# A normalised input written once by VectorE, its two parts formed by GpSimd ahead of slot 1, and a wait moved ahead of the experts

## The chip, the cores and the metric

One Trainium2 chip, one core of it. The metric is the time of one execution in microseconds (us). The engines run their own instruction streams side by side and wait for one another on semaphores: TensorE (PE) for matrix products into the accumulator memory PSUM, VectorE (DVE), ScalarE (ACT) and GpSimd (POOL) for elementwise work, SyncE (SP) for the DMA queue between HBM and the on-chip memory SBUF.

## What is computed

A block of three residual parts over 16 images of 64 channels by 256 positions: a graph convolution over the whole batch, a gated state-space scan over the positions, and a mixture of eight experts of which two count for each position. Cut to the last two, which the change touches:

```
t = t + scan(ln(t))                            # a recurrence over 256 positions, 128 channels x 16 states
logits = ln(t) @ Wr + br ; probs = softmax(logits) ; top_p, top_idx = top_k(probs, 2)
weights = top_p / top_p.sum(-1)
xn = (xt - mean) * rsqrt(var + eps)            # xt = ln(t)
h = gelu((xn * ln_g[e] + ln_b[e]) @ W1[e] + b1[e]) ; y[e] = h @ W2[e] + b2[e]     # e = 0..7
t = t + sum over the two chosen e of weights[e] * y[e]
```

## The kernel before

The kernel is written engine by engine, with every wait by hand; the order of each engine's stream is the order of its code. Two images, one of each half of the batch, are worked on at a time, 64 channels of each on 128 partitions, in G = 8 rounds. Round i runs the scan of pair i, the experts of the pair before (prev), and the input work of the two pairs after (nxt, nxt2). The loops are the four functions named body, one per engine; they call the same helpers in a fixed order.

The scan of a pair is cut into eight slots. dve_slot multiplies the input of two blocks into PSUM (L810) and runs the recurrence (L816) into the ring hs; pool_slot on GpSimd multiplies the result by Cs (L353, 128x1024); pe_sum adds four slots' worth on TensorE (L1117). When all slots are summed, dve_gate (L837) writes ygs, TensorE projects it, and dve_t1 (L841) makes t1, the state ahead of the experts. These are done one round later, between slot 0 and slot 1 of the next pair.

The layer norm ahead of the experts follows slot 1 on VectorE. dve_lnF (L847) writes tns for the router; dve_xn2 writes the experts' input. That input, X2, is held as a high part rounded to the matrix product's type and a low part, the rest, which are laid over each other on 128 partitions: the high part on partitions 0 to 63 (L862, for each half), the low part on 64 to 127 (L397, on GpSimd, from the unrounded copy xnt2 of L854). Both halves of the batch lie side by side in its 512 columns. The weights W1H and W1L stand on both halves of the partitions, so it does not matter on which half a part lies. The low part waits for both halves of the high part, for slot 1 of GpSimd and for the experts of the pair before.

dve_router1 (L867, L870) takes logits from PSUM; ScalarE makes their exponentials (act_router, L656); dve_router2 (L878 to L899) finds the two best. Its instructions from L890 on read small tiles in SBUF, rt and rv. After L899 GpSimd makes the weights (pool_router, L403 to L414), which TensorE transposes (pe_wt).

On TensorE, pe_spread (L1209) copies steps for the scan's decay, then one warm matmul (pe_warm, L1296), whose result nobody reads, waits for X2's low part (xl2), then come pe_c and the experts: pe_f1 (L1265, L1266), Gelu on ScalarE (L680, after loading its table at L731), pe_f2 (L1280). Behind the experts come pe_b (L1171, L1173), which waits until VectorE's slot 7 has read the old content, pe_dtz and the pe_sum's. step_input on GpSimd (L338, L340) writes what SP then stores to HBM and loads back for the next pair.

The last pair has its own path behind the loops: VectorE writes the low part itself (L1100).

Of the kernel before, what the change touches and what calls it, by code (L numbers as in the profile page):

```python
# [24 lines left out]
B, D, HW = 16, 64, 256  # L25
HALF = B // 2
G = HALF
T = 2 * HW
# [6 lines left out]
SLOTS = NBLK // 2  # L35
CHUNKS = 4
BY_PE = (8, 9, 10, 11, 12, 13, 14, 15)
EXP, FH = 8, 256
# [32 lines left out]
def build(nc, x, cW1, cb1, Wl, bl, Wr, Wf, bf, cW2, cb2, W_in, b_in, W_conv, b_conv, A_log, W_bc, b_bc,  # L71
# [10 lines left out]
    with ctx:  # L82
        def sb(name, shape, dt=fp32):
            return ctx.enter_context(nc.sbuf_tensor(name, shape, dt))
# [3 lines left out]
        def since(eng, name, count):  # L88

            if count <= 0:  # L90
                return
            eng.wait_ge(S[name], count)

        def so_far(g, ahead):

            return min(g + ahead, G)
# [69 lines left out]
        rs2 = sb("rs2s", [128, HW])  # L166
        rqs = sb("rqs", [128, HW])
        tns = sb("tns", [128, HW])
        xnt2 = sb("xnt2", [64, T])
        X2 = sb("X2", [128, T], f32r)  # L170
        rt = sb("rt", [128, 12, 4, EXP])
        rv = sb("rv", [128, 8, 4])
# [159 lines left out]
        def step_input(eng, by, g, p):  # L332

            eng.wait_ge(S["sp_ln"], g + 1)
            eng.wait_ge(S["sp_relu"], g + 1)
            since(eng, "dt_out", 16 * (g - 1))
            since(eng, "dlo", g - 1)
            by.tensor_tensor(dts[:, p, :], rl[:, :], sp[:, :], ALU.add).then_inc(S["dt"], 1)  # L338
            eng.wait_ge(S["dt"], g + 1)
            by.tensor_tensor(u[:, :], dts[:, p, :], xc[:, p, :], ALU.mult).then_inc(S["u"], 1)  # L340
# [50 lines left out]
        def pool_x2(eng, g):  # L391

            eng.wait_ge(S["xn2"], 2 * (g + 1))
            eng.wait_ge(S["xh2"], 2 * (g + 1))
            eng.wait_ge(S["cm"], min(SLOTS * (g + 1) + 2, SLOTS * G))
            since(eng, "acc", EXP * g)
            gp.tensor_tensor(X2[64:128, :], xnt2[:, :], X2[0:64, :], ALU.subtract).then_inc(S["xl2"], 1)  # L397

        def pool_router(eng, g):

# [16 lines left out]
        def _(eng):  # L417
# [79 lines left out]
            def body(i, p, nxt, nxt2, prev):  # L497
# [11 lines left out]
                    pool_restart(eng, 0, 1)  # L509
                if nxt is not None:  # L510
                    step_input(eng, gp, nxt, q)
                pool_slot(eng, i, p, 1)
                if prev is not None:
                    pool_x2(eng, prev)
                    pool_router(eng, prev)
                pool_slot(eng, i, p, 2)
                pool_slot(eng, i, p, 3)
# [331 lines left out]
        def dve_xn2(eng, g, between=None):  # L849
            eng.wait_ge(S["rq"], g + 1)  # L850
            since(eng, "xl2", g)
            for h in range(2):
                q = slice(64 * h, 64 * h + 64)
                v.tensor_tensor(xnt2[:, HW * h:HW * h + HW], P[q, XB, 0:HW], rqs[q, :], ALU.mult).then_inc(S["xn2"], 1)  # L854
            if between is not None:
                between()
            since(eng, "f1", EXP * KC * g)
            for h in range(2):
                q = slice(64 * h, 64 * h + 64)
                if h == 1 and between is None:  # L860
                    dve_router1(eng, g)
                v.tensor_tensor(X2[0:64, HW * h:HW * h + HW], P[q, XB, 0:HW], rqs[q, :], ALU.mult).then_inc(S["xh2"], 1)  # L862

        def dve_router1(eng, g):
            logits = P[:, XC, 0:4 * EXP].rearrange("p (c e) -> p c e", e=EXP)
# [55 lines left out]
        def _(eng):  # L921
# [127 lines left out]
            def body(i, p, nxt, nxt2, prev):  # L1049
# [16 lines left out]
                dve_slot(eng, i, 1)  # L1066
                if prev is not None:
                    dve_lnF(eng, prev)
                    dve_xn2(eng, prev)
                    dve_router2(eng, prev, nxt2)  # L1070
                dve_slot(eng, i, 2)
                if i == 0:
# [24 lines left out]
            dve_t1(eng, G - 1, 1)  # L1097
            dve_xn2(eng, G - 1, lambda: dve_lnF(eng, G - 1))
            eng.wait_ge(S["xh2"], 2 * G)
            v.tensor_tensor(X2[64:128, :], xnt2[:, :], X2[0:64, :], ALU.subtract).then_inc(S["xl2"], 1)  # L1100
            dve_router1(eng, G - 1)
            dve_router2(eng, G - 1)
            for e in range(EXP):
# [195 lines left out]
        def _(eng):  # L1299
# [121 lines left out]
            def body(i, p, nxt, nxt2, prev):  # L1421
# [23 lines left out]
                pe_spread(eng, i, 14)  # L1445
                pe_spread(eng, i, 15)
                if prev is not None:
                    eng.wait_ge(S["xl2"], prev + 1)
                    pe_warm(eng, 1 if nxt is not None else 2, XB)
                if nxt is not None:  # L1450
                    pe_c(eng, nxt)
                if prev is not None:
# [79 lines left out]
```

## Time and profile before

| | us |
|---|---|
| median of three runs | 395.5 |
| the three runs | 395.0, 395.5, 399.7 |
| the profiled execution, its own time | 399.41 |
| its span in the profile | 397.7 |
| busy: TensorE | 332.3 |
| busy: VectorE | 325.8 |
| busy: ScalarE | 277.2 |
| busy: GpSimd | 267.7 |

The span is the part of an execution that the profiler covers, from the first instruction to the last. Busy time is what an engine's instructions took; waits are not in it. A time for one instruction is given as start and length, both in us from the span's start; a bracket behind it says how long the engine stood before it, and which instruction ended that. Instructions of one engine overlap by up to 0.1 us, since the next one's start is recorded while the last one ends. The granted clock of TensorE is given as a share of 2.4 GHz; it has two levels, 2.4 and 1.2 GHz, so 0.9 is a mean over a stretch. The whole span has 0.924.

### The profile page before, as it was taken

What the parts mean: (1) busy time and instruction counts of PE and PEld (TensorE: products, weight loads), DVE (VectorE), ACT (ScalarE), POOL (GpSimd) and SP (SyncE); (2) the same over time, 40 slices, a digit from 0 to 9 for tenths busy, and PEclk for the clock granted to TensorE, in tenths of its full rate; (3) what the DMA queues carried; (4) which work ended last, traced back from release to release, by engine and by line L of the source; (5) the groups of instructions that cost most, each with busy time, mean ns of one, the idle gap of its engine ahead of it and who ended that gap; (6) DMA issues with size and microseconds to landing.
All of it is one profiled execution on the core that took longest, in us unless ns stands there. A gap on an engine that the chain in (4) does not pass through costs nothing. (4 is left out here: it accounts for less than half of the span.)

```text
span 397.7 us, 5508 instructions
## 1 busy us (share of the span) xinstructions
PE 332.3 (84%) x1674; PEld 182.6 (46%) x1674; DVE 325.8 (82%) x428; ACT 277.2 (70%) x465; POOL 267.7 (67%) x255
## 2 busy tenths in 40 slices
PE   0695897487899889987997899789869987999794
PEld 0475445232555345534544464445345524555462
DVE  2777466998899999989999999899999989993411
ACT  1002557589888977899789778997996778661462
POOL 8803503797569967985699589858985895692122
PEclk9996999559899969999999899999987997899698
DMA  7753059899899888859775997589859960000000
GB/s 190 221 118 47 2 140 217 208 222 223 205 218 232 200 214 208 178 129 226 171 176 140 228 210 177 129 188 221 190 126 216 220 163 3 2 2 13 0 0 15
DMA packets 21302, 59.54 MB, mean 150 GB/s; under 512 B 4989, under 2 KB 13337, under 8 KB 15385
## 3 DMA queue, kind: packets, MB, share of 16 engines
q1 hardware_dynamic: 20104, 58.35, 63.6%
q10 hardware_dynamic: 1168, 0.84, 0.9%
q8 instruction: 14, 0.23, 0.3%
q14 instruction: 16, 0.12, 0.1%
HBM read 53.94 MB, written 5.24 MB: 149 GB/s over the span
## 5 line engine op out<-in xcount | busy, mean ns | idle before, releaser
L353 POOL TENSOR_TENSOR hs<-hs,Cs 128x1024 f32<-128x1024 f32 x63 | 149.6, 2377 | 40.3 <-DVE hs L816 39.7
L816 DVE TENSOR_TENSOR_SCAN hs<-av,P 128x1024 f32<-128x1024 f32 x64 | 146.3, 2286 | 6.2 <-PE P L1117 2.9
L680 ACT ACTIVATE hb<-P,b1c 128x512 f32<-128x512 f32 x128 | 81.5, 686 | 21.3 <-PE P L1266 20.9
L810 DVE TENSOR_TENSOR P<-P,ub 128x1024 f32<-128x1024 f32 x62 | 76.0, 1226 | 3.2 <-DMA ub<-u_scratch 0.9
L1280 PE MATMUL P<-hb,W2s 128*64 128x256 f32 x512 | 69.9, 396 | 0.0
L1265 PE MATMUL P<-X,W1H 128*128 128x512 f32 x128 | 61.4, 480 | 2.4 <-ACT hb L680 2.3
L1266 PE MATMUL P<-X,W1L 128*128 128x512 f32 x128 | 53.9, 421 | 0.0
L617 ACT ACTIVATE av<-P,Aneg 128x510 f32<-128x510 f32 x68 | 43.7, 683 | 6.7 <-POOL rl L340 3.5
L1280 PEld LDWEIGHTS P<-hb,W2s 128*64 128x64 f32 x512 | 31.8, 138 | 31.2 <-issue 21.4
L617 ACT ACTIVATE av<-av,Aneg 128x510 f32<-128x510 f32 x60 | 38.3, 707 | 0.3 <-DMA av<-dt_scratch 0.2
L1209 PE MATMUL P<-D,selD 128*128 128x512 f32 x64 | 30.6, 521 | 9.1 <-ACT av L617 6.7
L1265 PEld LDWEIGHTS P<-X,W1H 128*128 128x128 f32 x128 | 26.1, 204 | 21.1 <-ACT hb L680 14.2
L1117 PE MATMUL P<-hs,selS 128*32 128x512 f32 x256 | 30.2, 598 | 2.1 <-POOL hs L353 2.1
L673 ACT ACTIVATE wbs<-P 128x512 f32<-128x512 f32 x32 | 19.1, 598 | 15.3 <-PE P L1245 15.3
L1266 PEld LDWEIGHTS P<-X,W1L 128*128 128x128 f32 x128 | 26.6, 208 | 5.2 <-issue 2.3
L367 POOL TENSOR_TENSOR accs<-accs,mes 128x512 f32<-128x512 f32 x21 | 26.9, 1283 | 2.4 <-DVE mes L917 2.4
L1296 PE MATMUL P<-W1H 128*128 128x512 f32 x47 | 17.2, 464 | 8.2 <-POOL X L397 8.2
L1209 PEld LDWEIGHTS P<-D,selD 128*128 128x128 f32 x64 | 12.7, 205 | 21.7 <-issue 20.4
L917 DVE TENSOR_TENSOR mes<-P,wbs 128x512 f32<-128x512 f32 x28 | 18.7, 667 | 0.2 <-PE P L1280 0.2
L1117 PEld LDWEIGHTS P<-hs,selS 128*32 128x32 f32 x256 | 6.9, 109 | 23.4 <-issue 12.7
L907 DVE SCALAR_TENSOR_TENSOR mes<-P,cols,wbs 128x256 f32<-128x256 f32 x8 | 3.5, 479 | 16.7 <-PE P L1280 8.8
L389 POOL TENSOR_TENSOR D<-dts,D 64x512 fp32r<-64x512 f32 x8 | 10.2, 1274 | 7.8 <-ACT D L600 6.9
(214 smaller groups left out, 522.1 us busy)
## 6 DMA issues: line engine op xcount, KB each, us to landing
ub<-u_scratch SPq DMA_DIRECT2D x31, 1024.0 KB, 10.8
av<-dt_scratch SPq DMA_DIRECT2D x15, 1024.0 KB, 7.1
dt_scratch<-dts SPq DMA_DIRECT2D x7, 256.0 KB, 2.8
u_scratch<-rl SPq DMA_DIRECT2D x7, 256.0 KB, 2.8
av<-in_L_conv_Wr SPq DMA_DIRECT2D x2, 576.0 KB, 7.0
av<-in_L_conv_Wl SPq DMA_DIRECT2D x2, 576.0 KB, 7.6
res<-in_x SPq DMA_DIRECT2D x4, 256.0 KB, 4.6
hb<-in_L_ffn_W SPq DMA_DIRECT2D x2, 512.0 KB, 5.8
```

The lines of the kernel that those rows point to most:

```text
L353: gp.tensor_tensor(hs[:, at, :, :], hs[:, at, :, :], rep(Cs[:, p, :], 1, 2), ALU.mult).then_inc(S["cm"], 1)
L367: done = gp.tensor_tensor(acc[:, :, :], prev, mes[:, at:at + 2, :], ALU.add)
L617: a_.activation(steps, dt_of, ACT.Exp, scale=Aneg[:, m:m + 1]).then_inc(S["aexp"], 1)
L673: a_.activation(wbs[:, 2 * r:2 * r + 2, :].rearrange("p e f -> p (e f)"), P[:, YS, :], ACT.Copy).then_inc(S["wb"], 1)
L680: a_.activation(hb[:, r % 4, :], P[:, (XA, XB)[r % 2], :], ACT.Gelu, bias=b1c[:, r:r + 1]).then_inc(S["gl"], 1)
L810: v.tensor_tensor(ring, rep(P[:, BB, :], 1, 2), ub[:, 2 * n:2 * n + 2, :], ALU.mult).then_inc(S["bm"], 1)
L816: v.tensor_tensor_scan(hs[:, (SLOTS * g + n) % RING].rearrange("p a t -> p (a t)"), av[:, 2 * n:2 * n + 2, :].rearrange("p a t -> p (a t)" ...
L1117: last = pe.matmul(P[32 * q:32 * q + 32, YS, :], selS[:, k, :], hs[:, (SLOTS * g + n) % RING, q % 2, :], start=(k == 0), stop=(k == 3))
L1209: pe.matmul(P[:, (YS, XA)[m % 2], :], selD[:, m - BY_PE[0], :], D2[:, :], start=True, stop=True).then_inc(S["dt_pe"], 1)
L1265: pe.matmul(P[:, bank, :], W1H[:, e, 128 * k:128 * k + 128], X2[:, :], start=True, stop=False)
L1266: pe.matmul(P[:, bank, :], W1L[:, e, 128 * k:128 * k + 128], X2[:, :], start=False, stop=True).then_inc(S["f1"], 1)
L1280: last = pe.matmul(P[64 * h:64 * h + 64, (XC, XD)[pair % 2], HW * (e % 2):HW * (e % 2) + HW], W2s[:, e, k, :], hb[:, r % 4, HW * h:HW * h ...
```

## The change

VectorE writes the unrounded input once, as one 128x256 multiply (dve_xn1) in the partitions that the halves have in PSUM, and no longer writes the rounded part. GpSimd forms both parts: two copies into X2 with rounding, each in its half's own partitions, and two subtractions into the other partitions. This piece (pool_x2) moves from behind slot 1 to ahead of it, and GpSimd waits for its completion (xl2) before slot 1. On TensorE the wait ahead of the warm matmul is now for xn2, the unrounded input, there are two warm matmuls in every round, and the wait for X2 is that of the first expert matmul. The last pair's path keeps its order.

```diff
-        xnt2 = sb("xnt2", [64, T])
+        xnt2 = sb("xnt2", [128, T])
+        xn = xnt2[:, 0:HW]
 ...
         def pool_x2(eng, g):
             eng.wait_ge(S["xn2"], 2 * (g + 1))
-            eng.wait_ge(S["xh2"], 2 * (g + 1))
-            eng.wait_ge(S["cm"], min(SLOTS * (g + 1) + 2, SLOTS * G))
-            since(eng, "acc", EXP * g)
-            gp.tensor_tensor(X2[64:128, :], xnt2[:, :], X2[0:64, :], ALU.subtract).then_inc(S["xl2"], 1)
+            since(eng, "f1", EXP * KC * g)
+            eng.wait_ge(S["u"], so_far(g, 3))
+            eng.wait_ge(S["cm"], SLOTS * (g + 1) + 1)
+            for h in range(2):
+                q = slice(64 * h, 64 * h + 64)
+                gp.tensor_copy(X2[q, HW * h:HW * h + HW], xn[q, :]).then_inc(S["xh2"], 1)
+            for h in range(2):
+                q, o = slice(64 * h, 64 * h + 64), slice(64 - 64 * h, 128 - 64 * h)
+                eng.wait_ge(S["xh2"], 2 * g + h + 1)
+                low = gp.tensor_tensor(X2[o, HW * h:HW * h + HW], xn[q, :], X2[q, HW * h:HW * h + HW], ALU.subtract)
+            low.then_inc(S["xl2"], 1)
 ...
+                if prev is not None:
+                    pool_x2(eng, prev)
+                    eng.wait_ge(S["xl2"], prev + 1)
                 pool_slot(eng, i, p, 1)
                 if prev is not None:
-                    pool_x2(eng, prev)
                     pool_router(eng, prev)
 ...
+        def dve_xn1(eng, g):
+            eng.wait_ge(S["rq"], g + 1)
+            since(eng, "xl2", g)
+            v.tensor_tensor(xn, P[:, XB, 0:HW], rqs[:, :], ALU.mult).then_inc(S["xn2"], 2)
 ...
                     dve_lnF(eng, prev)
-                    dve_xn2(eng, prev)
+                    dve_xn1(eng, prev)
+                    dve_router1(eng, prev)
                     dve_router2(eng, prev, nxt2)
 ...
                 if prev is not None:
-                    eng.wait_ge(S["xl2"], prev + 1)
-                    pe_warm(eng, 1 if nxt is not None else 2, XB)
+                    eng.wait_ge(S["xn2"], 2 * (prev + 1))
+                    pe_warm(eng, 2, XB)
```

GpSimd's stream around slot 1 of a round, before. hs<-hs,Cs is a slot's multiply (slot 0 at the top, slot 1 the next), X is X2, xnt is xnt2, the rt and vv rows are the router's weights.

```order
L353 TENSOR_TENSOR hs<-hs,Cs 128x1024
L338 TENSOR_TENSOR dts<-rl,sp 128x512
L340 TENSOR_TENSOR rl<-dts,xc 128x512
L353 TENSOR_TENSOR hs<-hs,Cs 128x1024
L397 TENSOR_TENSOR X<-xnt,X 64x512
L403 TENSOR_TENSOR rt<-rt,rv 128x32
L405 TENSOR_TENSOR rt<-rt 128x32
```

The same place after the change.

```order
L354 TENSOR_TENSOR hs<-hs,Cs 128x1024
L339 TENSOR_TENSOR dts<-rl,sp 128x512
L341 TENSOR_TENSOR rl<-dts,xc 128x512
L400 CAST X<-xnt 64x256 x2
L404 TENSOR_TENSOR X<-xnt,X 64x256 x2
L354 TENSOR_TENSOR hs<-hs,Cs 128x1024
L411 TENSOR_TENSOR rt<-rt,rv 128x32
L413 TENSOR_TENSOR rt<-rt 128x32
```

The formation of X, one instruction behind slot 1, has become four ahead of it; slot 1 now stands directly ahead of the router's first instruction.

VectorE's stream between the scans of slot 1 and slot 2, before; the rv and rt rows are the router.

```order
L847 TENSOR_TENSOR tns<-P,rs2s 128x256 [waits rs2]
L854 TENSOR_TENSOR xnt<-P,rqs 64x256 [waits rq]
L854 TENSOR_TENSOR xnt<-P,rqs 64x256
L862 TENSOR_TENSOR X<-P,rqs 64x256
L867 TENSOR_REDUCE rv<-P 128x4 [waits lg]
L870 TENSOR_TENSOR rt<-P,rv 128x32 [waits m1]
L862 TENSOR_TENSOR X<-P,rqs 64x256
L878 SCALAR_TENSOR_TENSOR P<-P,rank 128x32 [waits ex]
```

The same place after the change.

```order
L857 TENSOR_TENSOR tns<-P,rs2s 128x256 [waits rs2]
L877 TENSOR_TENSOR xnt<-P,rqs 128x256 [waits rq]
L882 TENSOR_REDUCE rv<-P 128x4 [waits lg]
L885 TENSOR_TENSOR rt<-P,rv 128x32 [waits m1]
L893 SCALAR_TENSOR_TENSOR P<-P,rank 128x32 [waits ex]
L895 TENSOR_REDUCE rv<-P 128x4 [waits s1]
L897 TENSOR_TENSOR rt<-P,rv 128x32 [waits ms1]
L899 SCALAR_TENSOR_TENSOR rt<-rt,P 128x32 [waits o1]
L901 TENSOR_REDUCE rv<-rt 128x4 [waits e2]
L832 TENSOR_TENSOR xnt<-P,rs 128x256 [waits g_mm,rs1]
L905 TENSOR_TENSOR rt<-rt,rv 128x32 [waits m2]
```

Four multiplies of 64x256 have become one of 128x256, and nothing stands between the router's L885 and L893, which waits for ScalarE's exponentials; L905 is L890 of the kernel before.

TensorE's stream at the head of the experts, before; the W1H row is the warm matmul, the Wrep row pe_c.

```order
L1209 MATMUL P<-D,selD 128x512 [waits aexp,dlo] x2
L1296 MATMUL P<-W1H 128x512 [waits xl2]
L1181 MATMUL P<-xc,Wrep 128x512 [waits aexp,xc]
L1265 MATMUL P<-X,W1H 128x512 [waits aexp,sp_relu,xl2]
L1266 MATMUL P<-X,W1L 128x512
```

The same place after the change.

```order
L1225 MATMUL P<-D,selD 128x512 [waits aexp,dlo] x2
L1312 MATMUL P<-W1H 128x512 [waits xn2]
L1312 MATMUL P<-W1H 128x512
L1197 MATMUL P<-xc,Wrep 128x512 [waits aexp,xc]
L1281 MATMUL P<-X,W1H 128x512 [waits aexp,sp_relu,xl2]
```

The wait for xl2 has moved past the warm matmul and pe_c to the first expert matmul, where it also stood before.

## Rows read from the trace of the kernel before

**Rows 1.** Busy time by window, round by round: length, PE, PEld, DVE, ACT, POOL, clock, DMA
```profile
101.98:139.33 37.35, 33.91 (x187) 17.75 (x185) 36.09 (x43) 33.31 (x58) 29.81 (x24) 1.00 0.92 213
139.33:179.11 39.78, 35.98 (x184) 19.14 (x184) 36.42 (x43) 33.44 (x58) 32.01 (x26) 0.91 0.79 183
179.11:216.65 37.54, 33.76 (x184) 17.64 (x184) 36.06 (x42) 33.43 (x58) 29.77 (x24) 1.00 0.78 179
216.65:255.93 39.28, 35.06 (x184) 18.69 (x184) 36.50 (x43) 33.29 (x58) 32.19 (x26) 0.96 0.79 185
...
293.26:330.58 37.32, 33.08 (x170) 17.22 (x170) 35.50 (x40) 28.22 (x49) 28.65 (x23) 0.91 0.81 187
330.58:362.41 31.83, 29.68 (x159) 16.12 (x159) 28.63 (x37) 18.84 (x31) 22.48 (x17) 0.89 0.01 1
```

**Rows 2.** Timeline of TensorE, rounds 3 and 4: start, length, instruction [idle before, releaser]
```profile
182.99 0.50 PE L1296 MATMUL P<-W1H 128*128 128x512 f32 x1 [0.99 <-POOL X L397]
...
204.69 0.50 PE L1171 MATMUL P<-ones,bhl 128*128 128x512 f32 x1 [0.29 <-DVE P L810]
...
220.96 0.80 PE L1296 MATMUL P<-W1H 128*128 128x512 f32 x1 [1.41 <-POOL X L397]
```

**Rows 3.** Timeline of ScalarE: first Gelu of rounds 3 and 4, exponentials of round 4
```profile
184.84 1.27 ACT L680 ACTIVATE hb<-P,b1c 128x512 f32<-128x512 f32 x2
...
218.79 0.23 ACT L656 ACTIVATE P<-rt 128x32 f32<-128x32 f32 x1
...
224.35 1.27 ACT L680 ACTIVATE hb<-P,b1c 128x512 f32<-128x512 f32 x2 [2.04 <-PE P L1266]
```

**Rows 4.** Timeline of all engines, end of round 7
```profile
358.20 1.23 DVE L1091 TENSOR_TENSOR hs<-hs,Cs 128x1024 f32<-128x1024 f32 x1
...
361.28 1.06 PE L1117 MATMUL P<-hs,selS 128*32 128x512 f32 x8
...
362.41 0.69 DVE L837 TENSOR_TENSOR ygs<-P,sg 128x512 f32<-128x512 f32 x1 [2.38 <-PE P L1117]
```

**Rows 5.** Timeline of VectorE, round 4, between the scans of slots 1 and 2
```profile
216.65 0.43 DVE L847 TENSOR_TENSOR tns<-P,rs2s 128x256 f32<-128x256 f32 x1
216.99 0.86 DVE L854 TENSOR_TENSOR xnt<-P,rqs 64x256 f32<-64x256 f32 x2
...
219.12 0.20 DVE L878 SCALAR_TENSOR_TENSOR P<-P,rank 128x32 f32<-128x32 f32 x1
...
220.47 0.49 DVE L890 TENSOR_TENSOR rt<-rt,rv 128x32 f32<-128x32 f32 x1
```

**Rows 6.** Timeline of GpSimd, round 4: slot 1, the low part of X, the router
```profile
217.04 2.37 POOL L353 TENSOR_TENSOR hs<-hs,Cs 128x1024 f32<-128x1024 f32 x1
219.64 1.26 POOL L397 TENSOR_TENSOR X<-xnt,X 64x512 fp32r<-64x512 f32 x1 [0.23 <-POOL hs L353]
221.77 0.24 POOL L403 TENSOR_TENSOR rt<-rt,rv 128x32 f32<-128x32 f32 x1 [0.87 <-DVE rt L899]
```

**Rows 7.** Timeline of VectorE: L890 of rounds 3 and 7
```profile
182.91 0.18 DVE L890 TENSOR_TENSOR rt<-rt,rv 128x32 f32<-128x32 f32 x1
...
334.18 0.41 DVE L890 TENSOR_TENSOR rt<-rt,rv 128x32 f32<-128x32 f32 x1
```

**Rows 8.** Timeline of GpSimd: the low part of X in round 7
```profile
333.28 1.26 POOL L397 TENSOR_TENSOR X<-xnt,X 64x512 fp32r<-64x512 f32 x1 [0.23 <-POOL hs L353]
```

**Rows 9.** Timeline of all engines in the start-up
```profile
30.88 3.61 POOL L480 TENSOR_TENSOR wbs<-hb,cols 128x2048 f32<-128x2048 f32 x1 [12.53 <-DMA hb<-in_L_ffn_W]
30.92 3.59 DVE L1002 TENSOR_SCALAR Aneg<-Aexp 128x16 f32<-128x16 f32 x1
```

**Rows 10.** Groups of GpSimd's instructions by shape: count, then busy us, mean ns, idle before
```profile
L384 POOL TENSOR_TENSOR accs<-accs,mes 128x256 f32<-128x256 f32 x7 | 5.1, 732 | 7.1 <-DVE mes L907 6.6
...
L412 POOL CAST vv<-rt 128x32 fp32r<-128x32 f32 x8 | 1.7, 211 | 0.5
...
L485 POOL CAST b2h<-mes 128x128 fp32r<-128x128 f32 x1 | 0.3, 292 | 0.0
```

More of the change, by code:

```diff
@@ L853, in dve_xn2 @@
                 q = slice(64 * h, 64 * h + 64)
-                v.tensor_tensor(xnt2[:, HW * h:HW * h + HW], P[q, XB, 0:HW], rqs[q, :], ALU.mult).then_inc(S["xn2"], 1)
+                v.tensor_tensor(xnt2[0:64, HW * h:HW * h + HW], P[q, XB, 0:HW], rqs[q, :], ALU.mult).then_inc(S["xn2"], 1)
             if between is not None:
@@ L1099, in _ @@
             eng.wait_ge(S["xh2"], 2 * G)
-            v.tensor_tensor(X2[64:128, :], xnt2[:, :], X2[0:64, :], ALU.subtract).then_inc(S["xl2"], 1)
+            v.tensor_tensor(X2[64:128, :], xnt2[0:64, :], X2[0:64, :], ALU.subtract).then_inc(S["xl2"], 1)
             dve_router1(eng, G - 1)
```

## The prediction

> **What bounds the kernel now.** I read the windows first, cut at the starts of tns (L847), one per image and round; rounds 1 to 4, 6 and 7 are in [rows 1], round 5 is like round 1. VectorE works 35.5 to 36.5 us of each of the first six, no engine more. Two kinds of round alternate: 1, 3, 5 and 6 take 37.3 to 37.5 us, 2 and 4 take 39.78 and 39.28 us at a granted clock of 0.91 and 0.96. The timelines say why. In round 4 TensorE stands 1.41 us before its warm matmul, which waits for the low part of X (L397, GpSimd) [rows 2]; that wait sits ahead of pe_c and of all experts. The warm matmul then takes 0.80 us, against 0.50 us in round 3 after a wait of 0.99 us: the clock has dropped from 2.4 to 1.2 GHz. So the first Gelu starts 7.70 us after tns in round 4 and 5.73 us in round 3 [rows 3], and VectorE pays behind it: it is idle for 3.4 us in the window of round 2 and 1.5 us in that of round 3 [rows 1].
>
> **What the change does, part by part.** *The moved wait.* TensorE now waits only for xn2, which the row of L854 puts near 217.4 us, long before TensorE is free, so the second warm matmul (0.50 us) lies in the stretch that is idle today and costs nothing. pe_c follows at once, and X is wanted only at the first expert matmul. This removes the low clock from rounds 2 and 4. It is worth at most their excess over 37.5 us, 2.3 and 1.8 us, if nothing new is late. In round 7 the wait before ygs, 2.38 us [rows 4], shrinks as well.
>
> *VectorE's edit.* One 128x256 multiply replaces four 64x256 ones of 0.43 us; by L847 (0.43 us, 128x256 too) three are saved, some 1.3 us a round. They are worth nothing: L878 needs an exp that ScalarE, busy until then, ran from 218.79 to 219.02 us [rows 3], and VectorE starts L878 at 219.12 us [rows 5]. Without the X multiplies it would stand until that same exp.
>
> *GpSimd's edit.* This decides. Today GpSimd runs slot 1 (2.37 us), then one 64x512 subtraction (1.26 us), then stands until L899 lets the router start [rows 6]. Afterwards it runs two copies and two subtractions of 64x256, waits for its own xl2, and only then runs slot 1; queued behind slot 1 are the router's weights, for which TensorE's transposes wait. Slot 1 comes to lie where GpSimd was subtracting or idle before: on top of L890 of VectorE's router.
>
> What that does is in the rows. L890 (rt and rv, both in SBUF) takes 0.18 us in round 3 [rows 7], where GpSimd's subtraction is over. In rounds 4 and 7 it takes 0.49 and 0.41 us and ends at 220.96 and 334.59 us [rows 5, 7]; L397 ends at 220.90 and 334.54 us [rows 6, 8], each time 0.05 or 0.06 us before. The start-up shows it at full length: L1002, on 128x16 elements, takes 3.59 us and ends with GpSimd's 3.61 us multiply L480 [rows 9]. So VectorE stands still for the rest of the GpSimd instruction. An instruction with an operand in PSUM doesn't: the two L854 of round 4 take 0.43 us each while slot 1 starts beside them.
>
> The Trainium skill says the same in "SBUF — State Buffer", section "SBUF: two separate sides": VectorE and GpSimd share one port pair as an exclusive lock, held for a whole instruction, and a VectorE instruction with two SBUF inputs needs it. By that rule the stall lasts to the end of slot 1 and the sum below stands; if a stall were never longer than the 0.3 us that L890 shows today, the kernel would gain and the first rival would be right. The trace agrees with the rule, with 3.59 us for L1002.
>
> **The sum.** First the stretch from tns to the end of L890, as it will be:
> 0.76 us to the end of the one multiply: 0.34 us from L847 to L854, then 0.42 us for 128x256.
> 0.14 us to reach GpSimd. A hand-over takes 0.07 us from TensorE to ygs (362.34 to 362.41 us [rows 4]) and 0.23 us before L397, which stands behind several waits [rows 6]; pool_x2 has four, so I take the middle.
> 2.26 us for the four new instructions. No 64x256 copy is in the trace; casts of 128x32 and 128x128 take 0.211 and 0.292 us [rows 10], 0.84 ns more for an element, so 0.40 us each. The subtractions are taken as L384 of 128x256, 0.73 us each.
> 0.10 us for the wait on its own xl2, between the same two ends, nearer the lower since only one wait is left open.
> 2.37 us for slot 1, and 0.05 us to the end of L890.
> This makes 5.68 us. VectorE asks for L890 3.82 us after tns (220.47 less 216.65), and slot 1 runs from 3.26 to 5.63 us after it, so L890 falls inside [rows 5]. Today L890 ends 3.98 us after tns in round 3 and 4.31 us in round 4.
>
> The rest of a round, from there to the next tns, is 37.54 less 3.98, 33.56 us, in round 3, and in round 1, whose L890 is as in round 3, 33.37 us. I take 33.4 us for every round, since the experts now start as early as in round 3. A new round is 33.4 + 5.68 = 39.08 us, six of them 234.5 us; now they take 330.58 less 101.98, 228.6 us: +5.9 us. Round 7 has the new 5.68 us, then 24.84 us from the end of L890 to that of VectorE's last multiply L1091 (359.43 us), then 1.13 us for the last sum, as from 361.28 to 362.41 us [rows 4]: 31.65 us against 31.83 us now, -0.2 us. Together +5.7 us on the profiled execution's 399.4 us: **405.1 us, say 405.0**.
>
> Nothing else is late in this sum. ScalarE, with the fast start, runs a round in 37.5 us (round 3), less than 39.08 us. GpSimd works 32.2 of 39.3 us in round 4 [rows 1] and gets about 1 us more. No DMA is moved, and step_input, which releases the scratch DMAs of SP, stays ahead of the moved work.
>
> How 399.4 us stands to the runs: three gave 395.0, 395.5 and 399.7 us, and the profiled execution is of the upper kind. The gap, 3.9 us to the median, is about the 4.1 us that rounds 2 and 4 lose, so I take it that the median run does not drop its clock there. A new round is set by VectorE and not by the experts, so 405.0 us holds for both kinds: 2.4% above the median.
>
> The Trainium skill ("TensorE: Matmul & The Clock Gate", section "What's actually happening") holds that the gate does not start over with the kernel, so one kernel changes its clock at other places from run to run. By it the two kinds of run are the clock's and 405.0 us stands; otherwise the median run would come out near 401 us, the last rival. One execution in the trace cannot show it.
>
> **Bounds of the unknown costs.** Copies no shorter than the cast of 128x32 (0.21 us) and subtractions no shorter than half of L397 (0.63 us) make 1.68 us: 0.58 us less in each of seven rounds, 401.0 us. All four at 0.73 us make 2.92 us: 0.66 us more, 409.7 us.
>
> **The rivals.**
> *The change works as it is written.* L890 runs beside slot 1, or slot 1 comes after it. Then rounds 2 and 4 fall to 37.5 us (-4.1 us), round 7 loses about 1.8 of its 2.38 us, and the kernel takes 393.5 us: not slower. Against it stand the rows of L890 and L1002. It decides at a stall of 0.84 us a round, 5.9 us of gain over seven stalls. Chance 0.09.
> *The clock drops at another place.* TensorE's L1171, behind the experts, waits for VectorE's multiply of slot 7, 0.29 us in round 3 [rows 2]. VectorE comes 1.7 us later there, so the wait grows to about 2 us, more than the 1.41 us after which the clock was low in round 4. Then pe_b, pe_dtz and the first sums run at half speed and the next scan waits for them, by about 2 us; in five rounds that makes 415 us. Against it: the engine comes from dense work there, and 0.99 us left the clock up. Chance 0.12.
> *The level lies elsewhere.* The stall is as I say, but the quick runs are quick for a reason outside rounds 2 and 4; then 5.7 us are added to 395.5: 401.2 us. Chance 0.22.
>
> **How the numbers follow.** The forecast has 0.52 (402 to 408 us by itself); 0.05 stays for what I don't see. The range, 398.5 to 409.5 us, takes in the bounds of the copies and the last rival with its own spread, and leaves out the first two, about 0.2. Two per cent of 395.5 us, about what a measurement of this kernel tells from no change, lies at 387.6 and 403.4 us. Slower: four fifths of the forecast, the clock, a little of the rest, 0.56. Same: 0.41. Faster: 0.03, since even the first rival stays within 2%.
>
> **What would show it.** In the new profile L905 (today's L890) should take about 2 us in each of rounds 1 to 7 and end 0.05 us after GpSimd's slot 1; tns should follow tns by some 39 us; the first Gelu should start about 5.7 us after tns in every round, at clock 1.00; VectorE should hardly wait for TensorE. I am wrong if L905 stays near 0.2 us, if slot 1 ends before or starts after it, or if the copies take other than 0.4 us.

## The result and the profile after

| | us |
|---|---|
| before: median of 4 runs | 395.94 (395.02 to 399.73) |
| after: median of 4 runs | 404.01 (402.95 to 404.32) |
| ratio of after to before | 1.0174, 95% interval 1.0131 to 1.0218 |
| after: the profiled execution, its own time | 402.95, span 401.1 |
| after: busy | TensorE 328.1, VectorE 326.6, ScalarE 278.4, GpSimd 274.7 |

The kernel became slower by 1.7%, with an interval that lies wholly above 1 and reaches past 1.02. Each ratio here is worked out from the runs that are at most 1.5% above the fastest of their kernel, and is not the quotient of the medians, which is 1.020 here. The prediction had 405.0 us, with a range of 398.5 to 409.5 us.

The windows of the kernel after, cut at the starts of tns (L857) as in [rows 1], for rounds 1, 4, 6 and 7. The columns are length, busy time of PE, PEld, DVE, ACT and POOL, clock, DMA share and GB/s.

```profile
100.28:139.26 38.98, 34.11 (x185) 17.67 (x185) 36.81 (x40) 33.59 (x58) 31.53 (x27) 1.00 0.90 205
...
217.23:256.21 38.98, 34.12 (x185) 17.69 (x185) 36.79 (x40) 33.58 (x58) 31.96 (x28) 1.00 0.77 179
...
295.18:334.22 39.04, 32.35 (x171) 16.23 (x171) 36.19 (x38) 28.24 (x49) 29.83 (x26) 0.96 0.77 179
334.22:366.02 31.80, 29.00 (x159) 15.29 (x159) 29.41 (x33) 19.02 (x31) 21.96 (x19) 0.95 0.01 2
```

Rounds 1 to 5 no longer differ: they take 38.97 to 38.99 us at clock 1.00, where [rows 1] had 37.35 to 39.78 us. VectorE is busy longer in a round (36.79 us in round 4, 36.50 us before) although it has three instructions fewer. From the first tns to the ygs of round 7 the kernel takes 366.02 less 100.28, 265.74 us; before it was 362.41 less 101.98, 260.43 us.

The timeline of VectorE in round 4, the answer to [rows 5]:

```profile
217.23 0.42 DVE L857 TENSOR_TENSOR tns<-P,rs2s 128x256 f32<-128x256 f32 x1
217.59 0.42 DVE L877 TENSOR_TENSOR xnt<-P,rqs 128x256 f32<-128x256 f32 x1
...
219.63 0.20 DVE L893 SCALAR_TENSOR_TENSOR P<-P,rank 128x32 f32<-128x32 f32 x1 [0.85 <-ACT P L666]
...
220.97 2.05 DVE L905 TENSOR_TENSOR rt<-rt,rv 128x32 f32<-128x32 f32 x1
222.94 0.16 DVE L906 TENSOR_SCALAR rv<-rv 128x4 f32<-128x4 f32 x1
```

And GpSimd's beside it, the answer to [rows 6]:

```profile
218.08 0.85 POOL L400 CAST X<-xnt 64x256 fp32r<-64x256 f32 x2 [0.43 <-DVE xnt L877]
219.00 1.53 POOL L404 TENSOR_TENSOR X<-xnt,X 64x256 fp32r<-64x256 f32 x2
220.61 2.37 POOL L354 TENSOR_TENSOR hs<-hs,Cs 128x1024 f32<-128x1024 f32 x1
223.84 0.24 POOL L411 TENSOR_TENSOR rt<-rt,rv 128x32 f32<-128x32 f32 x1 [0.86 <-DVE rt L914]
```

L905 works on 128x32 elements, as L890 did in 0.18 us [rows 7], and is recorded with 2.05 us. Slot 1 ends at 222.98 us and L905 at 223.02 us, 0.04 us behind it. In rounds 1 to 5 it takes 2.04 to 2.06 us, in rounds 6 and 7 2.37 and 2.33 us. In the profile such a stall counts as busy time: it has no bracket of idle time. Only the instruction's length, far out of line with its size, and its end just behind a GpSimd instruction give it away.

TensorE of rounds 4 and 6 and ScalarE of round 4, the answers to [rows 2, 3]:

```profile
219.96 0.62 PE L1312 MATMUL P<-W1H 128*128 128x512 f32 x2
...
222.90 1.27 ACT L690 ACTIVATE hb<-P,b1c 128x512 f32<-128x512 f32 x2
...
244.26 0.50 PE L1187 MATMUL P<-ones,bhl 128*128 128x512 f32 x1 [1.20 <-DVE P L820]
...
322.21 0.50 PE L1187 MATMUL P<-ones,bhl 128*128 128x512 f32 x1 [2.56 <-DVE P L820]
...
323.79 4.99 PE L1133 MATMUL P<-hs,selS 128*32 128x512 f32 x32
```

The wait ahead of the warm matmuls is gone, and the first Gelu starts 5.67 us after tns (222.90 less 217.23), where it took 7.70 us in round 4 of before. L1187 (L1171 before) now waits 1.20 us for the late VectorE, and the clock stays at 1.00 in that round. In round 6 it waits 2.56 us; it still takes 0.50 us itself, but the clock falls behind it: it is 0.50 from 323.25 to 326.50 us, and the 32 sums of L1133 take 4.99 us, where in round 4 they take 2.78 us for 24 and 1.07 us for 8. The round is hardly longer for it, 39.04 us.

### The profile page after: what moved, and what is told of

It reads as the page before. It is cut to its first block and busy times, and to the rows that moved or that the text cites. A ratio compares the mean times of both kernels' runs of the same rounds, so it can differ in the third digit from the quotient of the medians.

```text
span 401.1 us, 5528 instructions
## 1 busy us (share of the span) xinstructions
PE 328.1 (82%) x1680; PEld 177.0 (44%) x1680; DVE 326.6 (81%) x407; ACT 278.4 (69%) x465; POOL 274.7 (68%) x276
## 5 line engine op out<-in xcount | busy, mean ns | idle before, releaser
L1281 PE MATMUL P<-X,W1H 128*128 128x512 f32 x128 | 57.7, 451 | 3.7 <-ACT hb L690 3.6
L1282 PE MATMUL P<-X,W1L 128*128 128x512 f32 x128 | 51.9, 405 | 0.0
L627 ACT ACTIVATE av<-av,Aneg 128x510 f32<-128x510 f32 x60 | 38.2, 707 | 0.1
L1225 PE MATMUL P<-D,selD 128*128 128x512 f32 x64 | 29.6, 504 | 6.7 <-ACT av L627 4.2
L1133 PE MATMUL P<-hs,selS 128*32 128x512 f32 x256 | 31.7, 621 | 3.5 <-POOL hs L354 2.6
L1281 PEld LDWEIGHTS P<-X,W1H 128*128 128x128 f32 x128 | 24.7, 193 | 22.0 <-ACT hb L690 12.8
L1282 PEld LDWEIGHTS P<-X,W1L 128*128 128x128 f32 x128 | 24.9, 195 | 3.9 <-issue 1.0
L1133 PEld LDWEIGHTS P<-hs,selS 128*32 128x32 f32 x256 | 7.1, 113 | 27.2 <-issue 13.6
```

The costliest lines, as they stand in the source:

```text
L627: a_.activation(steps, dt_of, ACT.Exp, scale=Aneg[:, m:m + 1]).then_inc(S["aexp"], 1)
L1133: last = pe.matmul(P[32 * q:32 * q + 32, YS, :], selS[:, k, :], hs[:, (SLOTS * g + n) % RING, q % 2, :], start=(k == 0), stop=(k == 3))
L1225: pe.matmul(P[:, (YS, XA)[m % 2], :], selD[:, m - BY_PE[0], :], D2[:, :], start=True, stop=True).then_inc(S["dt_pe"], 1)
L1281: pe.matmul(P[:, bank, :], W1H[:, e, 128 * k:128 * k + 128], X2[:, :], start=True, stop=False)
L1282: pe.matmul(P[:, bank, :], W1L[:, e, 128 * k:128 * k + 128], X2[:, :], start=False, stop=True).then_inc(S["f1"], 1)
```

## The experiments

Two theories were put against each other first. Theory 1: a VectorE instruction that takes its inputs from SBUF, as L905 does, stands until the GpSimd instruction that is running has ended; the new place of slot 1 costs the stall. Theory 2: nothing is stalled by the engines' sharing, and the kernel is late because GpSimd itself is late: four instructions and a wait stand ahead of slot 1. Each ratio below is against runs of the kernel before on the same chip: 396.99 us (median of 23 runs) for the first four kernels, 397.27 us (25 runs) for the next four.

**Slot 1 behind the router.** The kernel after, with one GpSimd instruction moved and the wait on xl2 ahead of it left out:

```diff
                 if prev is not None:
                     pool_x2(eng, prev)
-                    eng.wait_ge(S["xl2"], prev + 1)
-                pool_slot(eng, i, p, 1)
-                if prev is not None:
                     pool_router(eng, prev)
+                pool_slot(eng, i, p, 1)
```

> The changed kernel with one move: GpSimd runs slot 1 behind the router's weights instead of ahead of them. Theory 1 (VectorE's instruction with two SBUF inputs stands until GpSimd's running instruction ends): nothing of GpSimd lies over L905 any more, so L905 takes 0.2 us instead of 2.05 us, a round falls from 39.0 to about 37.5 us, and the kernel to about 393.5 us, 10 us under the changed one. Theory 2 (GpSimd itself is late: four instructions and a wait ahead of slot 1): slot 1 comes still later, so no gain, 404 us or more.

391.79 us (390.09 to 393.57, 6 runs), ratio 0.9872 (0.9835 to 0.9909): 12.2 us less than the kernel after, and the lowest median of all. VectorE and GpSimd of its round 4:

```profile
214.62 0.42 DVE L855 TENSOR_TENSOR tns<-P,rs2s 128x256 f32<-128x256 f32 x1
...
217.01 0.20 DVE L891 SCALAR_TENSOR_TENSOR P<-P,rank 128x32 f32<-128x32 f32 x1 [0.85 <-ACT P L664]
...
218.35 0.18 DVE L903 TENSOR_TENSOR rt<-rt,rv 128x32 f32<-128x32 f32 x1
```
```profile
216.39 1.52 POOL L404 TENSOR_TENSOR X<-xnt,X 64x256 fp32r<-64x256 f32 x2
219.35 0.24 POOL L411 TENSOR_TENSOR rt<-rt,rv 128x32 f32<-128x32 f32 x1 [1.44 <-DVE rt L912]
...
220.81 4.72 POOL L354 TENSOR_TENSOR hs<-hs,Cs 128x1024 f32<-128x1024 f32 x2
```

L903 answers L905. GpSimd runs nothing while VectorE is in the router, and L903 takes 0.18 us. Rounds 1 to 5 take 37.25 to 37.30 us. From the first tns to the last ygs it is 252.97 us, 12.77 us less than after, or 1.8 us in each of seven rounds, about the 1.87 us (2.05 less 0.18) by which the instruction is shorter. Slot 1 starts 6.19 us after tns here, 3.38 us after it in the kernel after, and no round is longer for it. This refutes theory 2.

**TensorE's part alone.** The kernel before, with the wait moved and the second warm matmul:

```diff
-                    eng.wait_ge(S["xl2"], prev + 1)
-                    pe_warm(eng, 1 if nxt is not None else 2, XB)
+                    eng.wait_ge(S["xn2"], 2 * (prev + 1))
+                    eng.wait_ge(S["xh2"], 2 * (prev + 1))
+                    pe_warm(eng, 2, XB)
```

> The kernel before with TensorE's part alone: the warm matmuls (two) wait for VectorE's last write from the bank (xn2 and xh2), the low part is waited for at the first expert matmul. Theory 1, with the low clock in rounds 2 and 4 as the cause of the upper runs: clock 1.00 and 37.5 us in every round, first Gelu 5.8 us after tns, 393.5 us, with no runs near 399. If the two kinds of runs come from elsewhere: the rounds still fall, but the median goes to about 390 us with runs near 394 as well.

394.22 us (390.62 to 395.44, 12 runs), ratio 0.992 (0.9888 to 0.9952). Its windows of rounds 2 and 4:

```profile
138.42:175.76 37.34, 33.94 (x185) 17.81 (x185) 36.24 (x42) 33.36 (x58) 30.78 (x25) 1.00 0.81 187
...
213.57:251.01 37.44, 33.95 (x185) 17.82 (x185) 36.35 (x43) 33.41 (x58) 30.89 (x25) 1.00 0.83 186
```

The clock is 1.00 in rounds 1 to 6 and the two long rounds are gone. So TensorE's part is a gain by itself, which the kernel after spends on the stall and more; the moved wait and the second warm matmul were not tried one without the other. The median lies nearer the 393.5 us of the first theory than the 390 us of the second, and no run is near 399 us. But the twelve runs still spread over 4.8 us, so the two long rounds are not shown to be the whole of the spread before.

**X formed behind slot 1.** The kernel after, with pool_x2 back behind slot 1 and waiting for its end:

```diff
-            eng.wait_ge(S["cm"], SLOTS * (g + 1) + 1)
+            eng.wait_ge(S["cm"], min(SLOTS * (g + 1) + 2, SLOTS * G))
 ...
-                if prev is not None:
-                    pool_x2(eng, prev)
-                    eng.wait_ge(S["xl2"], prev + 1)
                 pool_slot(eng, i, p, 1)
                 if prev is not None:
+                    pool_x2(eng, prev)
                     pool_router(eng, prev)
```

> The changed kernel with the forming of X2 back behind slot 1 (two copies and two subtractions there, waiting for slot 1's end). Theory 1: slot 1 is over before L905, but the subtractions lie over the router: L905 is held by the first to about 4.3 us after tns, L908 (two SBUF inputs too) by the second to about 5.1 us; a round of about 38.3 us, 399.5 us. Theory 2: the wait ahead of slot 1 is gone, 393.5 to 395 us, with L905 and L908 at 0.2 us each.

397.75 us (394.23 to 398.6, 12 runs), ratio 1.0013 (0.9979 to 1.0046). Rounds of 37.9 us, between those of the first experiment and of the kernel after. VectorE's router in round 4 and the two subtractions beside it:

```profile
217.96 0.18 DVE L903 TENSOR_TENSOR rt<-rt,rv 128x32 f32<-128x32 f32 x1
...
218.18 0.68 DVE L906 TENSOR_TENSOR rt<-rt,rank 128x32 f32<-128x32 f32 x1
218.78 0.17 DVE L908 RECIPROCAL rv<-rv 128x4 f32<-128x4 f32 x1
218.89 0.19 DVE L910 TENSOR_REDUCE rv<-rt 128x4 f32<-128x32 f32 x1
219.11 0.53 DVE L912 TENSOR_TENSOR rt<-rt,rv 128x32 f32<-128x32 f32 x1
```
```profile
218.06 1.53 POOL L404 TENSOR_TENSOR X<-xnt,X 64x256 fp32r<-64x256 f32 x2
```

By halves of their row the two subtractions end at 218.83 and 219.59 us; L906 ends at 218.86 and L912 at 219.64 us, one stall for each. The expectation had the answer to L905 held by the first; that is L903, which started 0.10 us ahead of the subtraction and ran through in 0.18 us, and the instruction held was L906. Between the two stalls a reciprocal and a reduction with one input in SBUF run at full speed while the second subtraction is still on. So what stands depends on the VectorE instruction.

**Slot 1 in two halves.** The kernel after, with slot 1 as two 128x512 multiplies, so that an instruction that stands is freed earlier:

```diff
+            if n == 1 and g > 0:
+                gp.tensor_tensor(hs[:, at, 0, :], hs[:, at, 0, :], Cs[:, p, :], ALU.mult).then_inc(S["cmh"], 1)
+                gp.tensor_tensor(hs[:, at, 1, :], hs[:, at, 1, :], Cs[:, p, :], ALU.mult).then_inc(S["cmh"], 1)
+                eng.wait_ge(S["cmh"], 2 * g)
+                gp.memset(cmt[:, :], 0.0).then_inc(S["cm"], 1)
+                return
```

> The changed kernel with slot 1 on GpSimd cut into two instructions of 128x512 (about 1.28 us each), and a small fill that signals their end. Theory 1: L905 ends 0.05 us after the first half, about 0.9 us instead of 2.05, then L908 is held to the end of the second half; the kernel stays at 404 to 405 us. If L905 waits for slot 1 as a whole (its data or a port that stays taken between instructions): L905 still takes 2 us or more and L908 0.19 us, with the same time.

403.95 us (403.57 to 404.41, 4 runs), ratio 1.0183 (1.0147 to 1.0218): no quicker than the kernel after. Round 4:

```profile
221.83 0.95 DVE L912 TENSOR_TENSOR rt<-rt,rv 128x32 f32<-128x32 f32 x1
222.70 1.30 DVE L913 TENSOR_SCALAR rv<-rv 128x4 f32<-128x4 f32 x1
223.92 0.18 DVE L915 TENSOR_TENSOR rt<-rt,rank 128x32 f32<-128x32 f32 x1
```
```profile
221.46 1.27 POOL L356 TENSOR_TENSOR hs<-hs,Cs 128x512 f32<-128x512 f32 x1
222.69 1.29 POOL L357 TENSOR_TENSOR hs<-hs,Cs 128x512 f32<-128x512 f32 x1
```

L912 (the answer to L905) is freed by the first half, and the next instruction, L913, falls under the second: it ends at 224.00 us, the half at 223.98 us. The expectation had the second half hold the next multiply with two inputs (L915), which takes 0.18 us. L913 has a single input of 128x4 elements, so two inputs are not needed for a stall.

**The router's operands in PSUM.** The kernel after in its own order, with VectorE's intermediate results p5, p6, p7 and the second maximum p2 in free columns of PSUM. For that VectorE makes one reduction more, and TensorE's second expert products wait for the last mask (o2) where they waited for e2:

```diff
-            v.tensor_tensor(rt[:, 6], rt[:, 5], bc(2), ALU.is_equal).then_inc(S["s2"], 1)
-            v.tensor_scalar(rv[:, 4], rv[:, 2], 1.0, None, ALU.add).then_inc(S["den"], 1)
+            v.tensor_tensor(p6, p5, bc(2), ALU.is_equal).then_inc(S["s2"], 1)
+            v.tensor_scalar(rv[:, 4], p2, 1.0, None, ALU.add).then_inc(S["den"], 1)
```

> The changed kernel in its own order (slot 1 ahead of the router on GpSimd), but VectorE keeps the router's chances-without-the-best, the second mask and its ranked form in free columns of the XC bank of PSUM, and takes the second maximum once more into PSUM, so that no instruction of the router's second half has both inputs in SBUF, nor one input in SBUF and its output there through a scalar operation; one reduction of 128x32 more a round. Theory 1 (an instruction with two SBUF inputs, or a scalar one from SBUF to SBUF, stands until the GpSimd instruction that runs ends; one with an operand in PSUM doesn't): the answer to L905 takes 0.2 us although slot 1 runs on both sides of it, the last mask is ready about 4.1 to 4.5 us after tns instead of 6.5 us, GpSimd starts the router when slot 1 ends, some 5.8 us after tns, a round takes 37.3 to 37.5 us against 38.98 us in the changed kernel, and the time is about 392 us (ratio 0.985 to 0.995). Theory 3 (what stands is any VectorE instruction that uses SBUF, or the whole engine while slot 1 runs): 2 us at the same place, rounds of 39 us, about 404 us (ratio 1.017).

392.49 us (391.21 to 393.37, 4 runs), ratio 0.9896 (0.9845 to 0.9947). Round 4:

```profile
216.96 0.19 DVE L907 TENSOR_TENSOR P<-P,rv 128x32 f32<-128x32 f32 x1
217.06 0.15 DVE L909 TENSOR_SCALAR rv<-P 128x4 f32<-128x4 f32 x1
217.19 0.20 DVE L911 TENSOR_TENSOR P<-P,rank 128x32 f32<-128x32 f32 x1
...
217.65 0.19 DVE L917 TENSOR_TENSOR rt<-P,rv 128x32 f32<-128x32 f32 x1
```
```profile
216.49 2.38 POOL L354 TENSOR_TENSOR hs<-hs,Cs 128x1024 f32<-128x1024 f32 x1
218.82 0.24 POOL L411 TENSOR_TENSOR rt<-rt,rv 128x32 f32<-128x32 f32 x1
```

Slot 1 runs over the whole second half of the router, from 216.49 to 218.87 us, and nothing stands. Rounds 1 to 5 take 37.25 to 37.29 us, as in the first experiment. This is the most direct evidence for theory 1: the order on GpSimd, which theory 2 made the cause, is that of the kernel after, and slot 1 starts 3.37 us after tns as there. What differs is the place of VectorE's operands; the added reduction and the later wait are more work and more waiting, so the gain isn't theirs. The last mask (L917) is ready 4.72 us after tns, somewhat above the 4.1 to 4.5 us expected.

**A GpSimd instruction that only writes, and one that reads.** The first experiment's kernel with one more instruction between pool_x2 and the router:

```diff
                     pool_x2(eng, prev)
+                    eng.wait_ge(S["xl2"], prev + 1)
+                    since(eng, "f2", EXP * KC * prev)
+                    gp.memset(hb[:, 0:3, :], 0.0).then_inc(S["jk"], 1)
                     pool_router(eng, prev)
```

> The kernel of e1_slot1_behind_router with one more GpSimd instruction between the low parts of X and the router's weights: a memset of 128x1536 on the Gelu ring, which is not in use then. By the start-up's memsets (128x1024 in 0.956 us, 128x256 in 0.319 us) it takes about 1.4 us and lies from some 3.4 to 4.8 us after tns, over the instruction that answers L905, which VectorE asks for 3.7 us after tns. It writes SBUF and reads none. Theory 1a (only a GpSimd instruction that reads SBUF holds VectorE's two SBUF inputs back): 0.18 us there, rounds of 37.3 us, time as in e1_slot1_behind_router, 390 to 393.5 us. Theory 1b (any GpSimd instruction on SBUF holds them): about 1.1 us there, ending 0.05 us behind the memset, rounds of 38.1 to 38.2 us, about 398 us.

In both, ScalarE's first Gelu of a round waits for the new instruction, which uses Gelu's tile. In the second kernel the new line is a copy out of the experts' weights:

```diff
-                    gp.memset(hb[:, 0:3, :], 0.0).then_inc(S["jk"], 1)
+                    gp.tensor_copy(hb[:, 0:3, :].rearrange("p k f -> p (k f)"), W1H[:, 0:6, :].rearrange("p e f -> p (e f)")).then_inc(S["jk"], 1)
```

> As e6_memset_over_router, with a copy of 128x1536 out of the experts' weights (one input, in SBUF) in the memset's place. By the casts of 128x32 and 128x128 (0.211 and 0.292 us, 0.84 ns more for an element) and the 64x256 copies (0.43 us) about 1.4 us, at the same place. Theories 1a and 1b both: the answer to L905 takes about 1.1 us and ends 0.05 us behind the copy, rounds of 38.1 to 38.2 us, about 398 us. Theory 1c (only a GpSimd instruction with two inputs in SBUF holds VectorE): 0.18 us, rounds of 37.3 us, 390 to 393.5 us.

The memset: 394.68 us (393.65 to 396.16, 8 runs), ratio 0.995 (0.9913 to 0.9986), rounds of 37.78 us. The copy: 398.2 us (397.11 to 401.56, 8 runs), ratio 1.0053 (1.0007 to 1.0098), rounds of 38.06 us. The timeline of both engines in round 4, with the memset, then with the copy:

```profile
217.63 1.38 POOL L524 MEMSET hb<- 128x1536 f32 x1
...
218.02 0.18 DVE L908 TENSOR_TENSOR rt<-rt,rv 128x32 f32<-128x32 f32 x1
218.12 0.92 DVE L909 TENSOR_SCALAR rv<-rv 128x4 f32<-128x4 f32 x1
218.23 0.80 DVE L911 TENSOR_TENSOR rt<-rt,rank 128x32 f32<-128x32 f32 x1
```
```profile
219.73 1.47 POOL L524 COPY hb<-W1H 128x1536 f32<-128x1536 f32 x1
...
220.10 1.14 DVE L908 TENSOR_TENSOR rt<-rt,rv 128x32 f32<-128x32 f32 x1
221.16 0.16 DVE L909 TENSOR_SCALAR rv<-rv 128x4 f32<-128x4 f32 x1
```

Beside the copy, which has a single input, L908 stands to 221.24 us, 0.04 us behind the copy: as expected, and theory 1c (two inputs are needed on GpSimd's side) falls. Beside the memset L908 takes 0.18 us, as theory 1a had it. But the next instruction, L909, stands to 219.04 us, 0.03 us behind the memset's end, so the round came out at 37.78 us, where 1a had 37.3 and 1b 38.1 to 38.2 us: neither was right as a whole. In these rows an instruction with two inputs in SBUF is held by a GpSimd instruction that reads and passes beside one that only writes; TENSOR_SCALAR from SBUF to SBUF is held by one that only writes as well. The row of L911, with two inputs in SBUF, is recorded with 0.80 us beside the memset, to 219.03 us: it stands in line behind L909, so it doesn't show what would hold it by itself.

The Trainium skill ("SBUF — State Buffer", section "Who interferes with whom") makes just this distinction: two SBUF inputs contend with GpSimd's reads and not with one that only writes, and tensor_scalar contends where it enters a mode that takes the shared pair of ports. It also says that on trn2 a reduction never contends. The rows of L908 and of the third experiment's L910 agree; L909's fits, but no row shows which mode it was in.

**VectorE as before.** The kernel before with TensorE's moved wait, and on GpSimd the one subtraction ahead of the router and slot 1 behind it:

```diff
-                pool_slot(eng, i, p, 1)
                 if prev is not None:
                     pool_x2(eng, prev)
                     pool_router(eng, prev)
+                pool_slot(eng, i, p, 1)
```

> The order of e1_slot1_behind_router with the X of the kernel before: VectorE writes the normed input and the high part of X in four 64x256 multiplies (some 1.3 us a round more than the changed kernel's one), GpSimd makes only the one 64x512 subtraction, and TensorE waits as in the changed kernel. If VectorE's edit is worth nothing, because the instruction behind it waits for ScalarE's exp in either case: that wait of 0.85 us shrinks to about 0.1 us, rounds of 37.2 to 37.5 us as in e1_slot1_behind_router, 390 to 394 us. If the saved multiplies are worth their 1.3 us: rounds of 38.5 us, some 9 us more than e1_slot1_behind_router, about 400 us.

393.8 us (392.84 to 396.09, 10 runs), ratio 0.9912 (0.9877 to 0.9946); rounds 1, 2, 4 and 5 take 37.25 or 37.26 us, round 3 37.51 us. Round 4:

```profile
215.63 0.42 DVE L848 TENSOR_TENSOR tns<-P,rs2s 128x256 f32<-128x256 f32 x1
...
217.64 0.43 DVE L863 TENSOR_TENSOR X<-P,rqs 64x256 fp32r<-64x256 f32 x1
218.10 0.20 DVE L879 SCALAR_TENSOR_TENSOR P<-P,rank 128x32 f32<-128x32 f32 x1
```

With all four multiplies back the round is as long as in the first experiment. L879 starts 2.47 us after tns, and there its answer starts 2.39 us after tns: the saved 1.3 us went into the wait for ScalarE's exp. Round 7 takes 31.35 us, against 29.82 us in the first experiment, with the clock at 0.89 against 0.94; whether the multiplies have a part in that is open. The interval overlaps those of the first and the fifth experiment (0.987 and 0.990), so the three versions aren't told apart by their times.

**The kernel before, four more times.** The prediction had explained the spread of before's runs by the clock in rounds 2 and 4. Four single executions were profiled for it, unchanged.

> The kernel before, unchanged, for another profiled execution: where do its runs, 394 to 401.5 us, differ? Theory K (the prediction's: the clock in rounds 2 and 4): an execution at or under 396 us has rounds 2 and 4 at 37.3 to 37.6 us, one at 398 us or more has one or both at 39 us or more, and the first tns comes within 1 us of 102 us in all. Theory S (the start-up): rounds 2 and 4 are at 39.3 to 39.8 us in every execution, and the first tns moves with the time, over some 3 us, as it did over the kernels measured so far (100.3 to 103.6 us).

> A second execution of the kernel before, with the same two theories: K, quick executions lack the two long rounds; S, all have them and the first tns moves with the time.

> A third execution of the kernel before, with the same two theories: K, quick executions lack the two long rounds; S, all have them and the first tns moves with the time.

> A fourth execution of the kernel before, with the same two theories: K, quick executions lack the two long rounds; S, all have them and the first tns moves with the time.

| execution | us | first tns | rounds 1 to 5 |
|---|---|---|---|
| the one ahead of the prediction | 399.41 | 101.98 | 37.35, **39.78**, 37.54, **39.28**, 37.33 |
| b1 | 397.16 | 101.81 | **38.94**, 37.33, 37.65, 37.74, 37.47 |
| b2 | 397.64 | 101.48 | 37.41, 37.50, 37.56, **39.24**, **39.57** |
| b3 | 398.67 | 102.79 | 37.41, 37.50, 37.56, **38.98**, **38.77** |
| b4 | 400.16 | 102.81 | 37.34, **39.74**, 37.51, **39.26**, 37.32 |

The timeline of TensorE's warm matmul and the window of round 4 in b1, then the same of round 5 in b2:

```profile
220.01 0.50 PE L1296 MATMUL P<-W1H 128*128 128x512 f32 x1 [1.39 <-POOL X L397]
```
```profile
215.73:253.47 37.74, 33.67 (x184) 17.65 (x184) 36.38 (x44) 33.29 (x58) 31.16 (x25) 1.00 0.79 185
```
```profile
257.07 0.80 PE L1296 MATMUL P<-W1H 128*128 128x512 f32 x1 [0.99 <-POOL X L397]
```
```profile
253.19:292.76 39.57, 35.57 (x182) 18.77 (x182) 36.28 (x42) 33.44 (x58) 30.97 (x25) 0.91 0.77 177
```

Theory S falls: it had the long rounds in 2 and 4 always, and each execution has one or two long rounds, not the same ones. The long rounds are those of the lowered clock, as theory K had it, but K had them in rounds 2 and 4: in b1 the long round is round 1, in b2 and b3 one is round 5, and in b3 round 4 takes 38.98 us, where K asked for 39 us or more. K's main point, that an execution at or under 396 us has no long round, was not tested, since none of the four is that quick. Both the clock and the start-up have a part in the spread: between b1 and b4, 3.00 us apart, the stretch from the first tns to the last ygs differs by 2.26 us and the first tns by 1.00 us.

## Why the prediction was right, and where it was not

**The stall on slot 1: right.** It rested on L890 and L1002 ending with GpSimd's instruction [rows 7 to 9]. L905 ends 0.04 us behind slot 1, and the experiments that took slot 1 away from it, or took its operand out of SBUF, took the stall away, with the kernel's whole loss. One row was weaker support than the prediction made it: L1002, a TENSOR_SCALAR, has a single input in SBUF. It showed how long a stall can last, not that two inputs in SBUF cause one; L909 and L913 are of its kind.

**The terms of the sum.** In round 4, against 217.23 us, the start of tns:

| step | predicted | measured |
|---|---|---|
| to the end of the one multiply | 0.76 | 0.78 (218.01) |
| to GpSimd's first copy | 0.14 | 0.07 (218.08) |
| two copies, two subtractions | 2.26 | 2.45 (220.53) |
| wait on its own xl2 | 0.10 | 0.08 (220.61) |
| slot 1 | 2.37 | 2.37 (222.98) |
| to the end of the stalled instruction | 0.05 | 0.04 (223.02) |
| together | 5.68 | 5.79 |
| rest of the round | 33.4 | 33.19 |
| a round | 39.08 | 38.98 |
| round 7 to ygs | 31.65 | 31.80 |

The copies took 0.43 us each, for which 0.40 us had been worked out from smaller casts, and the subtractions 0.77 us where L384 of twice the partitions took 0.73 us. From the first tns to the last ygs, six predicted rounds and the seventh make 266.1 us; 265.74 us were measured.

The mechanism held for round 7 too. From the end of the stall to that of VectorE's last multiply (L1107, 364.83 us) it takes 24.84 us, as predicted, and from there to ygs 1.19 us, where 1.13 us was said.

**VectorE's edit: right, for the rounds.** L893 stands 0.85 us for ScalarE's exp, and with the four multiplies back rounds 1, 2, 4 and 5 are as long.

**The moved wait: right in kind.** With TensorE's part alone, rounds 2 and 4 fall to 37.34 and 37.44 us, where 37.5 us was said, and round 7 loses 1.53 us (31.83 to 30.30 us) of the 1.8 us given to it in the first rival. Over the medians it is worth 2.8 us (394.22 against 396.99 us), less than the 5.3 us by which that execution lies below the profiled one of before (255.09 against 260.43 us from the first tns to the last ygs). That profiled execution lost more than others: in b1 to b4 this stretch took 258.09 to 260.35 us.

**The reading of the clock: wrong in part.** The prediction took the wait of 1.41 us for what lowered the clock in round 4, and 0.99 us for harmless. In b1 a wait of 1.39 us leaves round 4 at clock 1.00; in b2 one of 0.99 us is followed by a warm matmul of 0.80 us and a round at 0.91. So the wait's length in one round does not decide. That the wait has a part in it holds: the kernel after and all eight variants have it moved, with a second warm matmul, and each keeps clock 1.00 in rounds 1 to 5, 45 rounds in all, where nine of the 25 of the kernel before are below. It is not the only place: in round 6 seven of these nine are at 0.91 to 0.96. Why the clock falls in one round and not in another stays open. The step that built on it, that the median run of before does not drop its clock, is not borne out, as far as the record goes: all five profiled executions, 397.16 to 400.16 us, drop it in one or two of rounds 1 to 5, and none was as quick as the median of 395.94 us.

**The absolute level: near, in part by luck.** The profiled execution of after took 402.95 us. The difference from first tns to last ygs, +5.31 us, on 399.41 us would be 404.72 us, but the first tns came 1.70 us earlier (100.28 against 101.98 us), which leaves 403.02 us. The prediction held the start-up for constant. Over 14 profiled executions of the kernels here the first tns came between 100.28 and 103.61 us, so this part varies by more than 3 us by itself. And the execution of before that the forecast was added to lay 3.5 us above its median of 395.94 us, while the profiled one of after lay 1.1 us below its own. So there is luck in coming within 1 us of the median of 404.01 us; what the working accounts for is the +5.7 us, against +5.31 us measured.

**The rivals.** The change as it is written, without a stall, was given 393.5 us; the experiments without the stall took 391.79 and 392.49 us, so the price was about right and the condition was not met. The clock dropping at L1171's wait did not come in rounds 1 to 5: the wait grew to 1.20 us (about 2 us was said) and the clock stayed at 1.00. In round 6, after 2.56 us, it came, as the rival had it, with the first sums at half speed, but the round took 39.04 us, 0.06 us more than the others, where the rival had 2 us. Nor does a wait of that length always bring it: in the kernel with the memset 2.57 us at the same place left round 6 at 1.00. The level elsewhere, 401.2 us, is 2.8 us short: the medians differ by 8.1 us, between the 5.7 us of that rival and the 9.5 us of the forecast. Against the longer series of before (medians 396.99 and 397.27 us) they differ by 7.0 and 6.7 us, so this rival is not settled.

## What to carry to other kernels

A GpSimd instruction that is moved is not only late or early for whoever waits for it: while it runs and reads SBUF, VectorE instructions with two SBUF inputs stand, however small, and a small TENSOR_SCALAR from SBUF to SBUF stood as well. So lay it beside VectorE work that reads PSUM, or keep VectorE's small operands there. The stall has no wait in the profile; look for small instructions whose length doesn't fit their size and that end just behind a GpSimd instruction. And an edit that saves work ahead of a wait for another engine lengthens the wait by as much and saves nothing there, however busy the engine looks.

## What the hardware showed that was not expected

TENSOR_SCALAR with a single input of 128x4 elements in SBUF stood 0.92 us for a memset, which reads nothing, while the TENSOR_TENSOR with two SBUF inputs just ahead of it passed in 0.18 us. A reciprocal with one SBUF input (0.17 us) was not held beside a GpSimd subtraction. Halving the GpSimd instruction brought nothing, since the second half caught the next instruction in line (0.95 and 1.30 us, together more than the 2.05 us of the one stall). TensorE's clock fell after a wait of 0.99 us in one round and not after one of 1.39 us in another; behind the experts it fell after one of 2.56 us and not after one of 2.57 us in another kernel. Why is open.
